# One softmax bias per query tile in place of one for the whole sequence, in a fused attention and feed-forward kernel

## The chip, the cores and the metric

The kernel runs on all eight cores of one Trainium2 chip, each core on its own sequence of the batch of eight; the cores exchange nothing. The metric is the device time in microseconds (us) of the slowest core.

## What is computed

One layer in pre-norm order: a causal attention with 16 heads of 64, then a feed-forward block with ternary weights, activations quantised per token, and a depthwise convolution of width 3 between the two products. The parts that matter here are the attention and the order of the two:

```python
# x: (8, 2048, 1024)
def attn(x, W_query, W_key, W_value):        # H = 16, DH = 64
    q, k, v = (heads(x @ W) for W in (W_query, W_key, W_value))
    scores = jnp.einsum('bhqd,bhkd->bhqk', q, k)
    scores = jnp.where(causal, scores, -jnp.inf)
    weights = jax.nn.softmax(scores / jnp.sqrt(jnp.float32(DH)), axis=-1)
    return merge(jnp.einsum('bhqk,bhkd->bhqd', weights, v))

x = x + attn(_layernorm(x), W_query, W_key, W_value)
x = x + ffn(_layernorm(x), w1, conv_w, conv_b, w2)
```

A softmax doesn't change when the same number is subtracted from all the scores of a query. The kernel subtracts a bound on the scores, so that the exponentials stay finite, and never looks for a row's true maximum.

## The kernel before, in words

The program is written out in full, without loops on the chip. Small functions marked `sec_t`, `sec_v`, `sec_s`, `sec_g`, `sec_sq` and `sec_gq` each append instructions to one engine (PE, DVE, ACT, POOL, the SyncE DMA queue, the GpSimd DMA queue), and each engine runs its list in the order written. All instructions go through the helper `emit` (line 75), so nearly every row of the profile carries that line and is told apart by its tile. On DVE, ACT and POOL `emit` also makes each instruction wait until the one before it on the same engine is complete:

```python
        if self.chain and self.n > 0:
            self.wait((self.sem, self.n))
```

The stages are:

1. Projections. 16 tiles of 128 rows of x are normalised (on ACT a pair Ln, Exp of one column of `smalls` gives the reciprocal root) and transposed, and Q, K and V are made into `qT`, `kT` and `vaug`, which stay in SBUF.
2. Norms and the bias (lines 465 to 555). For Q (`wix` 0) and K (`wix` 1) and each of four blocks `n` of 512 tokens, DVE squares the block into `sqb` in two halves, PE sums it over channels into one row of `psN`, and a `tensor_reduce` writes the block's largest squared norm into `nrm`, column `8 * wix + n`. Then a serial chain makes one number: two reductions over the four blocks, a product, Ln and Exp on ACT (a square root), two small `tensor_scalar` on DVE (times 0.125, at most 80, negated), a matmul with a row of ones that spreads it over 128 partitions of `psN`, and a `tensor_copy` into column 6 of `smalls` (token `expbias`).
3. Attention. For four query tiles `t` of 512 rows and eight head pairs `hp`: `emit_sc` puts the scores of a key chunk `kc` into `psS` (PE), `emit_exp1` turns them into `PT` (ACT, with `bias=smalls[:, 6:7]`, after a wait on `expbias` in `exp_pvwaits`), DVE masks the diagonal chunks, and `flush_pv` runs the product with V of the head pair before (`psPV`) and adds the result to `x1st`. After each head pair `emit_wsteps(2)` appends two steps of the work on the weights: sums of absolute values on ACT (`mk_w1_abs`, `mk_w2_abs`: a 1 MB load into one of the two halves of `wbuf`, then an Abs on ACT; load `i` waits for Abs `i - 2`), and after those the ternary quantisation on DVE.
4. Feed-forward. After a barrier on all that went before, eight groups of 256 tokens go through `psM`, the convolution (`tmpc`, `cbuf`), the sigmoid, the quantisation (`amx`, `hsil`, `hq`) and `psO`.

On PE the order around the change is: the norm matmuls of `sqb`, the matmul that spreads the bias (`psN<-nrm,onesrow_s`), and behind it the first scores `psS` of t = 0, hp = 0. On ACT it is: the last Ln and Exp of stage 1, Ln and Exp of the bias, the four exponentials of t = 0, hp = 0, two Abs of `wbuf`.

Of the kernel before, what the change touches and what calls it, by code (L numbers as in the profile page):

```python
# [10 lines left out]
AF = mybir.ActivationFunctionType  # L11
ALU = mybir.AluOpType
AX = mybir.AxisListType
# [9 lines left out]
NQT = S // QTW  # L23
# [108 lines left out]
def build_program(debug=False):  # L132
# [23 lines left out]
    dbg = {}  # L156
# [15 lines left out]
    with es:  # L172
# [11 lines left out]
        onesrow = es.enter_context(nc.sbuf_tensor("onesrow_s", [1, 128], F32))  # L184
        convw = es.enter_context(nc.sbuf_tensor("convw_s", [128, 96], F32))
        convb = es.enter_context(nc.sbuf_tensor("convb_s", [128, 32], F32))
        smalls = es.enter_context(nc.sbuf_tensor("smalls", [128, 64], F32))
# [262 lines left out]
        with esA2:  # L450
# [67 lines left out]
                            "tensor_reduce", nrm[0:1, col:col + 1],  # L518
                            psN[0:1, 0:512], AX.X, ALU.max)

            @sec_v
            def _(ve):
                VE.emit("tensor_reduce", nrm[0:1, 16:17], nrm[0:1, 0:4],
                        AX.X, ALU.max)
                VE.emit("tensor_reduce", nrm[0:1, 17:18], nrm[0:1, 8:12],
                        AX.X, ALU.max)
                toks["c2"] = VE.emit(
                    "tensor_tensor", nrm[0:1, 18:19], nrm[0:1, 16:17],
                    nrm[0:1, 17:18], ALU.mult)

            @sec_s
            def _(se):
                SE.wait(toks["c2"])
                SE.emit("activation", out=nrm[0:1, 19:20],
                        in_=nrm[0:1, 18:19], func=AF.Ln)
                toks["cval"] = SE.emit(
                    "activation", out=nrm[0:1, 20:21],
                    in_=nrm[0:1, 19:20], func=AF.Exp, scale=0.5)

            @sec_v  # L540
            def _(ve):
                VE.wait(toks["cval"])
                VE.emit("tensor_scalar", nrm[0:1, 21:22], nrm[0:1, 20:21],
                        0.125, 80.0, ALU.mult, ALU.min)
                toks["negb"] = VE.emit(
                    "tensor_scalar_mul", nrm[0:1, 22:23], nrm[0:1, 21:22],
                    -1.0)

            @sec_t
            def _(te):  # L550
                TE.wait(toks["negb"])
                TE.emit("matmul", psN[:, 0:1], onesrow[0:1, :],
                        nrm[0:1, 22:23], start=True, stop=True)
                toks["negb_mm"] = TE.tok()

            @sec_v
            def _(ve):
                VE.wait(toks["negb_mm"])
                toks["expbias"] = VE.emit(
                    "tensor_copy", smalls[:, 6:7], psN[:, 0:1])  # L560

            if debug:
                @sec_v
                def _(ve):
                    toks["dbg_nb"] = VE.emit("tensor_copy", nrm[0:1, 32:39],
                                             nrm[0:1, 16:23])

                @sec_sq
                def _(sy):
                    SQ.emit("dma_start", out=dbg["d_nb"][0:1, 0:7],  # L570
                            in_=nrm[0:1, 32:39], waits=[toks["dbg_nb"]])

            def mk_w1_abs(i):
                c, hf = divmod(i, 2)
# [257 lines left out]
            for t in range(NQT):  # L832
# [4 lines left out]
                for hp in range(8):  # L837
# [28 lines left out]
                            toks[("sc", t, hp, kc)] = TE.tok()  # L866

                    def exp_pvwaits(t, hp, kc):
                        SE.wait(toks["expbias"])
                        if kc == 0:  # L870
                            if hp >= 2:
                                SE.wait(toks[("pv", t, hp - 2, 0)])
                                SE.wait(toks[("pv", t, hp - 2, 1)])
                            elif t >= 1:
                                SE.wait(toks[("pv", t - 1, 6 + hp, 0)])
                                SE.wait(toks[("pv", t - 1, 6 + hp, 1)])

                    def emit_exp1(t, hp, kc):
                        hpar = kc % 2

                        @sec_s
                        def _(se, t=t, hp=hp, kc=kc, hpar=hpar):
                            SE.wait(toks[("sc", t, hp, kc)])
                            exp_pvwaits(t, hp, kc)
                            c0 = max(0, (kc - 4 * t) * 128)
                            bP = psS[hpar]
                            src_ap = bP[:].rearrange(
                                "p (h w) -> p h w", w=QTW)[:, :, c0:QTW]
                            PTp = PT[:, (hp % 2) * 2 * PTW:
                                      (hp % 2 + 1) * 2 * PTW]  # L890
                            dst_ap = PTp.rearrange(
                                "p (h w) -> p h w", w=16 * 512)[
                                :, :, 512 * kc + c0:512 * (kc + 1)]
                            toks[("exp", t, hp, kc)] = SE.emit(
                                "activation", out=dst_ap, in_=src_ap,
                                func=AF.Exp, scale=0.125,
                                bias=smalls[:, 6:7])

                    def emit_exp2(t, hp, kc):
                        @sec_s  # L900
                        def _(se, t=t, hp=hp, kc=kc):
# [12 lines left out]
                            tok = SE.emit(  # L914
                                "activation", out=dst_ap, in_=src_ap,
                                func=AF.Exp, scale=0.125,
                                bias=smalls[:, 6:7])
                            toks[("exp", t, hp, kc)] = tok
                            toks[("exp", t, hp, kc + 1)] = tok

# [663 lines left out]
```

How the kernel before makes its waits and increments, by code:

```python
    def wait(self, tok):  # L52
        if tok is None:
            return
        if isinstance(tok, list):
            for t in tok:
                self.wait(t)
            return
        sem, val = tok
        if val <= 0:
            return
        key = id(sem)
        if self._waited.get(key, -1) >= val:
            return
        if not DRY[0]:
            self.raw.wait_ge(sem, val)
        self._waited[key] = val
# [1 line left out]
    def emit(self, name, *a, waits=(), **kw):  # L69
        if self.chain and self.n > 0:
            self.wait((self.sem, self.n))
        for t in waits:
            self.wait(t)
        if not DRY[0]:
            inst = getattr(self.raw, name)(*a, **kw)
            inst.then_inc(self.sem, 1)
        self.n += 1
        return (self.sem, self.n)
# [20 lines left out]
    def wait(self, tok):  # L99
        if tok is None:
            return
        if isinstance(tok, list):
            for t in tok:
                self.wait(t)
            return
        sem, val = tok
        if val <= 0:
            return
        key = id(sem)
        if self._waited.get(key, -1) >= val:
            return
        if not DRY[0]:
            self.raw.wait_ge(sem, val)
        self._waited[key] = val
# [1 line left out]
    def emit(self, name, *a, waits=(), **kw):  # L116
# [5 lines left out]
        if not DRY[0]:  # L122
            inst = getattr(self.raw, name)(*a, **kw)
            inst.then_inc(self.sems[j], 16)
        self.counts[j] += 16
```

## Time and profile before

| | us |
|---|---|
| two timed runs | 2157.40, 2158.38 (median 2157.89) |
| profiled execution, its own time | 2155.54 |
| its span on the slowest core (core 1) | 2154.0 |
| spans of the eight cores | 2140.8 to 2154.0 |
| stage 1, to the last V matmul | 0 to about 323 |
| stage 2, norms and bias | about 324 to 388 |
| stage 3, attention and weights | about 388 to 1005 |
| stage 4, feed-forward | about 1005 to 2154 |

All rows are of core 1 unless a number of another core is named, and times in them count from the start of its span. The profiled execution took 1.54 us more than the span. Its time is 2.35 us under the median of the timed runs.

### The profile page before, as it was taken

The page shows a single profiled execution, that of the slowest core. Times are in us where ns is not written, and L with a number is a line of the kernel's source. Part 1 is how long each engine was busy: PE and PEld are TensorE (multiplying, and loading weights), DVE is VectorE, ACT ScalarE, POOL GpSimd, SP SyncE. Part 2 cuts the span into 40 slices and gives each one's busy share as a digit, 9 for nine tenths or more (in the row PEclk, how much of TensorE's full clock was granted, in tenths as well). Part 3 has the DMA queues.
Part 4 walks back from the last instruction along what each step waited for, and adds up shares of the span by engine and source line. Part 5 has one row for each costly group of instructions (what it writes and reads, how often), then busy time and mean ns, then how long its engine had stood idle before and what let it go on. Part 6 is the DMA issues. An engine that isn't in the chain of part 4 may idle for free.

```text
span 2154.0 us, 23769 instructions; the slowest of 8 cores (2140.8 to 2154.0 us)
## 1 busy us (share of the span) xinstructions
PE 1084.5 (50%) x7038; PEld 596.5 (28%) x7038; DVE 1058.6 (49%) x2042; ACT 829.2 (38%) x904; POOL 280.9 (13%) x255
## 2 busy tenths in 40 slices
PE   0656784344454445550042437355273564757555
PEld 0322330122232222330031324233232332443422
DVE  1344434333345556653545646547455474666560
ACT  3100000677855556750243251542424514252612
POOL 0000000000000000000012312213113231242320
PEclk9977885555665556665566768788686786989887
DMA  7211002474444454436522321323203223142300
GB/s 233 63 39 40 20 1 78 157 233 159 160 114 130 135 174 147 140 130 200 188 88 88 108 69 59 102 75 105 91 20 127 89 72 95 61 136 78 118 20 20
DMA packets 108273, 224.03 MB, mean 104 GB/s; under 512 B 4593, under 2 KB 70258, under 8 KB 104050
## 3 DMA queue, kind: packets, MB, share of 16 engines
q1 hardware_dynamic: 94962, 172.18, 25.7%
q0 software_dynamic: 13184, 50.34, 6.8%
q8 instruction: 58, 0.95, 0.2%
q14 instruction: 69, 0.57, 0.1%
HBM read 188.94 MB, written 33.55 MB: 103 GB/s over the span
## 4 chain that ended last, share of the span: by engine, by line
DVE 34%; PE 22%; DMA 17%; ACT 14%; issue 10%; DVEq 1%; SPq 1%; ACTq 0%; POOL 0%; POOLq 0%
PE psQK L75 8%; DMA wbuf<-w1t 7%; PE psO L75 6%; DVE t1s L75 5%; DVE amx L75 5%; DVE hsil L75 4%; DVE smalls L75 4%; DMA wbuf<-w2t 4%; PE psM L75 3%; DMA x1t<-x1scr 3%; ACT hf L75 3%; DVE cbuf L75 3%; DVE tmpc L75 3%; ACT PT L75 3%; ACT hq L75 2%
## 5 line engine op out<-in xcount | busy, mean ns | idle before, releaser
L75 PE MATMUL psM<-xqT,t1b 128*128 128x258 bf16 x2048 | 324.3, 327 | 369.8 <-DVE cbuf L75 357.4
L75 ACT ACTIVATE PT<-psS,smalls 128x1024 bf16<-128x1024 f32 (+1 forms) x320 | 315.5, 986 | 179.8 <-PE psS L75 152.1
L75 PEld LDWEIGHTS psM<-xqT,t1b 128*128 128x128 bf16 x2048 | 230.2, 116 | 463.0 <-issue 401.0
L75 ACT ACTIVATE tmpc<-psM,convb_s,convw_s 128x256 f32<-128x256 f32 x256 | 144.5, 565 | 386.1 <-PE psM L75 257.1
L75 PE MATMUL psS<-qT,kT 64*128 64x512 bf16 x640 | 168.3, 532 | 218.1 <-ACT PT L75 218.1
L75 PE MATMUL psO<-t2T,hq 128*128 128x512 bf16 x1024 | 224.1, 381 | 34.7 <-ACT hq L75 34.7
L75 DVE SCALAR_TENSOR_TENSOR tmpc<-psM,convw_s,tmpc 128x256 f32<-128x256 f32 x256 | 123.7, 483 | 233.4 <-ACT tmpc L75 211.8
L75 POOL TENSOR_TENSOR hsil<-cbuf,hsil 128x1024 f32<-128x1024 f32 x64 | 150.6, 2353 | 537.5 <-ACT hsil L75 537.5
L75 PE MATMUL psPV<-vaug,PT 128*128 128x65 bf16 x2176 | 117.0, 237 | 69.2 <-DVE PT L75 69.2
L75 ACT ACT_TABLE_LOAD x26 | 33.4, 1283 | 288.8 <-DVE smalls L75 162.0
L75 PEld LDWEIGHTS psO<-t2T,hq 128*128 128x128 bf16 x1024 | 100.1, 98 | 157.3 <-issue 39.4
L75 DVE SCALAR_TENSOR_TENSOR cbuf<-psM,convw_s,tmpc 128x256 f32<-128x256 f32 x256 | 123.7, 483 | 27.1 <-DVE tmpc L75 0.5
L75 PEld LDWEIGHTS psPV<-vaug,PT 128*128 128x128 bf16 x2176 | 112.9, 128 | 83.7 <-issue 83.7
L75 PEld LDWEIGHTS psS<-qT,kT 64*128 64x128 bf16 x640 | 37.2, 99 | 334.5 <-issue 332.1
L75 DVE TENSOR_REDUCE amx<-hsil 128x256 f32<-128x8192 f32 x8 | 112.7, 14089 | 4.7 <-POOL hsil L75 3.9
L75 DVE TENSOR_SCALAR t1s<-wbuf,smalls 128x2048 bf16<-128x2048 f32 x32 | 41.2, 1286 | 130.5 <-DMA wbuf<-w1t 70.5
L75 ACT ACTIVATE smalls<-smalls 128x1 f32<-128x1 f32 x64 | 13.0, 203 | 229.5 <-DVE smalls L75 226.1
L75 DVE TENSOR_TENSOR hsil<-hsil,s2row 128x256 f32<-128x256 f32 x128 | 92.5, 723 | 14.1 <-DVE hsil L75 0.9
L75 POOL TENSOR_TENSOR hsil<-hsil,s2row 128x256 f32<-128x256 f32 x128 | 93.9, 734 | 40.6 <-DVE s2row L75 22.3
L75 ACT ACTIVATE hsil<-cbuf 128x1024 f32<-128x1024 f32 x64 | 67.6, 1057 | 54.3 <-DVE cbuf L75 52.1
L75 DVE SCALAR_TENSOR_TENSOR x1st<-psPV,recb,x1st 128x64 f32<-128x64 f32 x256 | 72.5, 283 | 27.5 <-DVE x1st L75 0.9
L123 POOL DMA_DIRECT2D x1scr<-x1st x4 | 3.0, 750 | 622.6 <-DVE PT L75 331.8
(80 smaller groups left out, 1159.5 us busy)
## 6 DMA issues: line engine op xcount, KB each, us to landing
t1b<-t1scr SPq DMA_DIRECT2D x64, 1024.0 KB, 5.6
wbuf<-w1t SPq DMA_DIRECT2D x32, 1024.0 KB, 6.6
wbuf<-w2t SPq DMA_DIRECT2D x32, 1024.0 KB, 6.0
xstage<-x POOLq DMA_DIRECT2D x16, 512.0 KB, 4.1
x1st<-x POOLq DMA_DIRECT2D x4, 2048.0 KB, 11.4
x1scr<-x1st POOLq DMA_DIRECT2D x4, 2048.0 KB, 9.8
t1scr<-t1s SPq DMA_DIRECT2D x16, 512.0 KB, 3.8
t2scr<-t1s SPq DMA_DIRECT2D x16, 512.0 KB, 3.2
```

The source lines that it names most:

```text
L75: inst = getattr(self.raw, name)(*a, **kw)
L123: inst = getattr(self.raw, name)(*a, **kw)
```

## The change

The single chain of stage 2 goes, and a function `emit_bias(t)` takes its place. It is called four times in a row, for t = 0 to 3, where the single chain stood, before the first score matmul of the attention. Each call makes a bias for one query tile, from the largest squared norm of Q in block t and the largest of K over blocks 0 to t (a running maximum in columns 24 to 27 of `nrm`). The four results go to columns 6, 14, 15 and 29 of `smalls`, and the exponentials of tile t wait for and use their own. Every call has its own cells in `nrm` and `psN`. Nothing else is moved. The part under `debug`, cut below, isn't built.

```diff
@@ -518,57 +518,61 @@
                             "tensor_reduce", nrm[0:1, col:col + 1],
                             psN[0:1, 0:512], AX.X, ALU.max)
 
-            @sec_v
-            def _(ve):
-                VE.emit("tensor_reduce", nrm[0:1, 16:17], nrm[0:1, 0:4],
-                        AX.X, ALU.max)
-                VE.emit("tensor_reduce", nrm[0:1, 17:18], nrm[0:1, 8:12],
-                        AX.X, ALU.max)
-                toks["c2"] = VE.emit(
-                    "tensor_tensor", nrm[0:1, 18:19], nrm[0:1, 16:17],
-                    nrm[0:1, 17:18], ALU.mult)
-
-            @sec_s
-            def _(se):
-                SE.wait(toks["c2"])
-                SE.emit("activation", out=nrm[0:1, 19:20],
-                        in_=nrm[0:1, 18:19], func=AF.Ln)
-                toks["cval"] = SE.emit(
-                    "activation", out=nrm[0:1, 20:21],
-                    in_=nrm[0:1, 19:20], func=AF.Exp, scale=0.5)
-
-            @sec_v
-            def _(ve):
-                VE.wait(toks["cval"])
-                VE.emit("tensor_scalar", nrm[0:1, 21:22], nrm[0:1, 20:21],
-                        0.125, 80.0, ALU.mult, ALU.min)
-                toks["negb"] = VE.emit(
-                    "tensor_scalar_mul", nrm[0:1, 22:23], nrm[0:1, 21:22],
-                    -1.0)
-
-            @sec_t
-            def _(te):
-                TE.wait(toks["negb"])
-                TE.emit("matmul", psN[:, 0:1], onesrow[0:1, :],
-                        nrm[0:1, 22:23], start=True, stop=True)
-                toks["negb_mm"] = TE.tok()
-
-            @sec_v
-            def _(ve):
-                VE.wait(toks["negb_mm"])
-                toks["expbias"] = VE.emit(
-                    "tensor_copy", smalls[:, 6:7], psN[:, 0:1])
-
-            if debug:
+            BCOL = [6, 14, 15, 29]
+
+            def emit_bias(t):
                 @sec_v
...
+                def _(ve, t=t):
+                    VE.wait(toks[("nrm_rd", 0, t)])
+                    VE.wait(toks[("nrm_rd", 1, t)])
+                    if t == 0:
+                        VE.emit("tensor_copy", nrm[0:1, 24:25],
+                                nrm[0:1, 8:9])
+                    else:
+                        VE.emit("tensor_tensor", nrm[0:1, 24 + t:25 + t],
+                                nrm[0:1, 23 + t:24 + t],
+                                nrm[0:1, 8 + t:9 + t], ALU.max)
+                    toks[("c2", t)] = VE.emit(
+                        "tensor_tensor", nrm[0:1, 44 + t:45 + t],
+                        nrm[0:1, t:t + 1], nrm[0:1, 24 + t:25 + t],
+                        ALU.mult)
+
+                @sec_s
+                def _(se, t=t):
+                    SE.wait(toks[("c2", t)])
+                    SE.emit("activation", out=nrm[0:1, 48 + t:49 + t],
+                            in_=nrm[0:1, 44 + t:45 + t], func=AF.Ln)
+                    toks[("cexp", t)] = SE.emit(
+                        "activation", out=nrm[0:1, 52 + t:53 + t],
+                        in_=nrm[0:1, 48 + t:49 + t], func=AF.Exp, scale=0.5)
+
+                @sec_v
+                def _(ve, t=t):
+                    VE.wait(toks[("cexp", t)])
+                    VE.emit("tensor_scalar", nrm[0:1, 56 + t:57 + t],
+                            nrm[0:1, 52 + t:53 + t], 0.125, 80.0,
+                            ALU.mult, ALU.min)
+                    toks[("negb", t)] = VE.emit(
+                        "tensor_scalar_mul", nrm[0:1, 60 + t:61 + t],
+                        nrm[0:1, 56 + t:57 + t], -1.0)
+
+                @sec_t
+                def _(te, t=t):
+                    TE.wait(toks[("negb", t)])
+                    TE.emit("matmul", psN[:, 2 + t:3 + t], onesrow[0:1, :],
+                            nrm[0:1, 60 + t:61 + t], start=True, stop=True)
+                    toks[("negb_mm", t)] = TE.tok()
+
+                @sec_v
+                def _(ve, t=t):
+                    VE.wait(toks[("negb_mm", t)])
+                    toks[("expbias", t)] = VE.emit(
+                        "tensor_copy", smalls[:, BCOL[t]:BCOL[t] + 1],
+                        psN[:, 2 + t:3 + t])
+
+            for t in range(NQT):
+                emit_bias(t)
+
 
             def mk_w1_abs(i):
                 c, hf = divmod(i, 2)
@@ -866,7 +870,7 @@
                             toks[("sc", t, hp, kc)] = TE.tok()
 
                     def exp_pvwaits(t, hp, kc):
-                        SE.wait(toks["expbias"])
+                        SE.wait(toks[("expbias", t)])
                         if kc == 0:
                             if hp >= 2:
                                 SE.wait(toks[("pv", t, hp - 2, 0)])
@@ -894,7 +898,7 @@
                             toks[("exp", t, hp, kc)] = SE.emit(
                                 "activation", out=dst_ap, in_=src_ap,
                                 func=AF.Exp, scale=0.125,
-                                bias=smalls[:, 6:7])
+                                bias=smalls[:, BCOL[t]:BCOL[t] + 1])
 
                     def emit_exp2(t, hp, kc):
                         @sec_s
@@ -914,7 +918,7 @@
                             tok = SE.emit(
                                 "activation", out=dst_ap, in_=src_ap,
                                 func=AF.Exp, scale=0.125,
-                                bias=smalls[:, 6:7])
+                                bias=smalls[:, BCOL[t]:BCOL[t] + 1])
                             toks[("exp", t, hp, kc)] = tok
                             toks[("exp", t, hp, kc + 1)] = tok
 
```

DVE, from the last reduction of the norms (`nrm<-psN`) to the first mask of the attention (`PT<-PT,mask_s`), before:

```order
L75 TENSOR_REDUCE nrm<-psN 1x1
L75 TENSOR_REDUCE nrm<-nrm 1x1 x2
L75 TENSOR_TENSOR nrm<-nrm 1x1
L75 TENSOR_SCALAR nrm<-nrm 1x1 x2
L75 COPY smalls<-psN 128x1
L75 TENSOR_TENSOR PT<-PT,mask_s 128x128 x8
```

and now:

```order
L75 TENSOR_REDUCE nrm<-psN 1x1
L75 COPY nrm<-nrm 1x1
L75 TENSOR_TENSOR nrm<-nrm 1x1
L75 TENSOR_SCALAR nrm<-nrm 1x1 x2
L75 COPY smalls<-psN 128x1
L75 TENSOR_TENSOR nrm<-nrm 1x1 x2
L75 TENSOR_SCALAR nrm<-nrm 1x1 x2
L75 COPY smalls<-psN 128x1
...
L75 TENSOR_TENSOR PT<-PT,mask_s 128x128 x8
```

The group of five rows that begins with two TENSOR_TENSOR stands three times (t = 1, 2, 3); the line of dots stands for the second and third of them. DVE gains 14 small instructions in all.

PE and ACT at the same place, as a difference (PE first: the matmul that spreads the bias, between the norms and the scores):

```order
 L75 MATMUL psN<-sqb,onesb_s 1x512 x64
-L75 MATMUL psN<-nrm,onesrow_s 128x1
+L75 MATMUL psN<-nrm,onesrow_s 128x1 x4
 L75 MATMUL psS<-qT,kT 128x512 x16
```

```order
 L234 UNCONDITIONAL_BRANCH
-L75 ACTIVATE nrm<-nrm 1x1 x2
+L75 ACTIVATE nrm<-nrm 1x1 x8
 L75 ACTIVATE PT<-psS,smalls 128x2x512
 L75 ACTIVATE PT<-psS,smalls 128x2x384
```

PE has three more small matmuls ahead of the first scores, and ACT six more one-element activations ahead of the first exponential. POOL and the SyncE queue are as before.

## Rows read from the trace of the kernel before

**Rows 1.** The page's chain that ended last, shares of the span by engine and tile.

```profile
DVE 34%; PE 22%; DMA 17%; ACT 14%; issue 10%; DVEq 1%; SPq 1%; ACTq 0%; POOL 0%; POOLq 0%
```

**Rows 2.** DVE in order of time, 383.5 to 389: start, duration, then the idle before it.

```profile
383.56 0.68 DVE L75 TENSOR_REDUCE nrm<-psN 1x1 f32<-1x512 f32 x1 [2.19 <-PE psN L75]
384.34 0.39 DVE L75 TENSOR_REDUCE nrm<-nrm 1x1 f32<-1x4 f32 x2
384.84 0.15 DVE L75 TENSOR_TENSOR nrm<-nrm 1x1 f32<-1x1 f32 x1
387.08 0.39 DVE L75 TENSOR_SCALAR nrm<-nrm 1x1 f32<-1x1 f32 x2 [2.09 <-ACT nrm L75]
388.34 0.16 DVE L75 COPY smalls<-psN 128x1 f32<-128x1 f32 x1 [0.88 <-PE psN L75]
```

**Rows 3.** ACT in order of time, 384 to 389.5.

```profile
385.12 1.28 ACT L75 ACT_TABLE_LOAD   x1 [108.80 <-DVE nrm L75]
386.41 0.49 ACT L75 ACTIVATE nrm<-nrm 1x1 f32<-1x1 f32 x2
388.95 1.11 ACT L75 ACTIVATE PT<-psS,smalls 128x1024 bf16<-128x1024 f32 x1 [2.04 <-PE psS L75]
```

**Rows 4.** PE in order of time, 383 to 389.

```profile
387.61 0.55 PE L75 MATMUL psN<-nrm,onesrow_s 1*128 1x1 f32 x2 [4.23 <-DVE nrm L75]
388.10 1.03 PE L75 MATMUL psS<-qT,kT 64*128 64x512 bf16 x4
```

**Rows 5.** ACT, then the SyncE queue, in order of time from 391.

```profile
392.53 1.91 ACT L75 ACTIVATE wbuf<-wbuf 128x2048 f32<-128x2048 f32 x1
394.35 0.19 ACT L75 ACTIVATION_READ_ACCUMULATOR wbuf<-wbuf 128x1 f32 x1
...
400.98 1.91 ACT L75 ACTIVATE wbuf<-wbuf 128x2048 f32<-128x2048 f32 x1 [0.77 <-DMA wbuf<-w1t]
...
394.62 12.58 SPq L123 DMA_DIRECT2D wbuf<-w1t  x4
```

**Rows 6.** DVE and ACT in order of time in stage 1, around one Ln and Exp.

```profile
257.06 0.15 DVE L75 TENSOR_SCALAR smalls<-smalls 128x1 f32<-128x1 f32 x1
258.03 0.16 DVE L75 SCALAR_TENSOR_TENSOR smalls<-smalls 128x1 f32<-128x1 f32 x1 [0.82 <-ACT smalls L75]
258.49 0.81 DVE L75 TENSOR_SCALAR lnstage<-xstage,smalls 128x1024 bf16<-128x1024 f32 x1 [0.30 <-DVE smalls L75]
...
257.36 0.50 ACT L75 ACTIVATE smalls<-smalls 128x1 f32<-128x1 f32 x2 [51.11 <-DVE smalls L75]
263.64 0.50 ACT L75 ACTIVATE smalls<-smalls 128x1 f32<-128x1 f32 x2 [5.79 <-DVE smalls L75]
```

**Rows 7.** ACT by groups, 0 to 1040: count, busy and mean ns, idle before.

```profile
L75 ACT ACTIVATE smalls<-smalls 128x1 f32<-128x1 f32 x36 | 7.3, 203 | 211.7 <-DVE smalls L75 209.7
...
L75 ACT ACT_TABLE_LOAD x3 | 3.8, 1283 | 188.4 <-DVE nrm L75 108.8 <-DVE smalls L75 64.2 <-DMA wstage<-wq 15.4
```

**Rows 8.** Busy time by stretch (PE, PEld, DVE, ACT, POOL), then granted clock, DMA share, GB/s.

```profile
380.00:388.00 8.00, 2.25 (x6) 0.79 (x6) 2.62 (x7) 1.69 (x3) 0.00 (x0) 0.50 0.00 0
388.00:400.00 12.00, 5.21 (x26) 1.50 (x27) 1.96 (x9) 10.14 (x12) 0.00 (x0) 0.50 0.28 96
440.00:460.00 20.00, 6.81 (x56) 3.03 (x56) 10.84 (x46) 17.07 (x19) 0.00 (x0) 0.50 0.69 248
388.00:1040.00 652.00, 285.39 (x2837) 153.04 (x2837) 311.22 (x715) 384.18 (x391) 7.09 (x12) 0.58 0.51 163
1040.00:2154.00 1114.00, 579.31 (x3240) 348.10 (x3240) 600.47 (x1088) 412.63 (x465) 263.41 (x221) 0.77 0.26 83
```

**Rows 9.** The chain that ended last, 1040 to 2154: shares by engine and tile.

```profile
by line: issue 11.5%; PE psO L75 11.4%; DVE amx L75 10.1%; DVE hsil L75 8.3%; PE psM L75 6.4%; DVE smalls L75 6.4%; ACT hf L75 5.5%; DMA x1t<-x1scr 5.2%; DVE tmpc L75 5.0%; DVE cbuf L75 5.0%; ACT hq L75 4.0%; ACT hsil L75 3.1%; ACT tmpc L75
```

**Rows 10.** Spans and mean granted TensorE clock by core; then cores 0 and 4 at the bias.

```profile
core 0: 2149.4 us, clock 0.715
...
core 4: 2145.1 us, clock 0.716
core 5: 2140.8 us, clock 0.716
...
383.68 0.39 DVE L75 TENSOR_REDUCE nrm<-nrm 1x1 f32<-1x4 f32 x2
...
386.15 0.39 DVE L75 TENSOR_REDUCE nrm<-nrm 1x1 f32<-1x4 f32 x2
```

More of the change, by code:

```diff
@@ L549, in _ @@
-            @sec_t
-            def _(te):
-                TE.wait(toks["negb"])
-                TE.emit("matmul", psN[:, 0:1], onesrow[0:1, :],
-                        nrm[0:1, 22:23], start=True, stop=True)
-                toks["negb_mm"] = TE.tok()
-            @sec_v
-            def _(ve):
-                VE.wait(toks["negb_mm"])
-                toks["expbias"] = VE.emit(
-                    "tensor_copy", smalls[:, 6:7], psN[:, 0:1])
-            if debug:
-                @sec_v
[L564 to L571, printed above, removed]
+            BCOL = [6, 14, 15, 29]
```

## The prediction, written before the changed kernel ran

> **What bounds the kernel now.** I read first the page's chain that ended last [rows 1]. It is spread over DVE, PE, DMA and ACT, none above 34%: the kernel is a relay in which one engine hands to the next, and no engine has a queue of work that would hide a delay. So the question is local: at the place of the change, is the work on that relay, and does anything after it run by a time of its own?
>
> Next I read each engine in order of time at the bias. DVE ends the last norm reduction at 384.24 and starts the old chain at 384.34 [rows 2]. ACT had been idle for 108.80 us when it takes the chain up at 385.12 [rows 3]; PE was idle for 4.23 us before the matmul that spreads the bias at 387.61, and starts the first scores at 388.10, directly behind it [rows 4]; the first exponential starts at 388.95, having waited for the scores [rows 3]. From 384.34 to 388.95 exactly one engine works at a time, each named as the releaser of the next. The whole chain is on the path, 4.6 us. Only the last copy into `smalls` (388.34 to 388.50) has 0.45 us to spare, because the scores are longer.
>
> **The change, part by part.** *First bias (t = 0).* Two reductions and a product become a copy and a product. The two reductions start at 384.34 and the product at 384.84 [rows 2], so one such step is 0.25 us with its self-wait. One step fewer: -0.25 us.
>
> *Three more biases.* Each further chain starts on DVE only after the copy of the chain before it, since DVE runs its list in order and that copy is written first. So the chains can't overlap, although the numbers they need are all there at 384.24. One round costs, start to start:
> - copy into `smalls` to the running maximum: one DVE step, 0.25
> - running maximum to product: one DVE step, 0.25
> - product to Ln: 384.84 to 385.12, 0.28 in front of the table load [rows 2, 3]; without a load in front it is 257.06 to 257.36, 0.30 [rows 6]. I take 0.28
> - Ln to the first `tensor_scalar`, over Exp: 386.41 to 387.08, 0.67 [rows 2, 3]; the same in stage 1, 257.36 to 258.03 [rows 6]
> - the two `tensor_scalar` to the matmul: 387.08 to 387.61, 0.53 [rows 2, 4]
> - matmul (it shows as two passes, 0.55 in all) to the copy: 387.61 to 388.34, 0.73 [rows 2, 4]
>
> The sum is 0.25 + 0.25 + 0.28 + 0.67 + 0.53 + 0.73 = 2.71 us a round, and 8.13 us for three.
>
> Every operation in a round has a row of before at the same shape; only the maximum has none of its own, and is taken as the product beside it, also a `tensor_tensor` on one element (0.15 us). Bounds for a round: up, DVE once needs 0.46 us from step to step in stage 1 (258.03 to 258.49) where the chain shows 0.25 [rows 6]; with that at each of the four times that a DVE instruction of a round waits for the one before it, it is 2.71 + 4 x 0.21 = 3.55. Down, if the 0.18 us between the end of the matmul (387.61 + 0.55) and the copy (388.34) were nothing, 2.53. I take 2.71, since it is made of the rows at this very place; the ends give 7.6 and 10.65 for three.
>
> *What stands behind it on each engine.* On PE the first scores of t = 0 are queued behind all four spreading matmuls, and on ACT the first exponential behind all eight Ln and Exp. Before, the time from the matmul to the first exponential was 388.95 - 387.61 = 1.34 us; it stays so after the last of them. The bias for t = 0 is ready early and nobody can use it. The waits on `("expbias", t)` in the attention then cost nothing: all four biases are complete before the first exponential could start.
>
> *The table load.* ACT loads a table once, at 385.12, and then runs Ln, Exp and all the exponentials of the attention with it: only three loads stand between 0 and 1040, one in each of stages 1, 2 and 4, although stage 1 has 16 pairs Ln, Exp [rows 7], which follow one another without a load [rows 6]. So I count no further load.
>
> *Does the delay reach the end?* The work that could be waiting on something else is the loading of `w1t`. Its first two loads have been in since stage 2. The next is issued at 394.62, when the first Abs is through (394.35 + 0.19), and the Abs of its data starts at 400.98 [rows 5]. That Abs is queued on ACT behind the first four exponentials, so the loads move with the bias. The DMA share is 0.00 from 380 to 388 [rows 8]: there is no transfer in flight that would be waited for anyway. All later stages hang on attention, and stage 4 on a barrier. Nothing is hidden.
>
> *Clock.* The granted clock is 0.50, the lower level (1.2 GHz), in the 8 us before the attention and still at 440 to 460 [rows 8]. A longer pause of PE at this place has nothing to take away.
>
> **Sum.** 3 x 2.71 - 0.25 = +7.9 us. The profiled execution took 2155.54 and would take 2163.4; the median of the timed runs is 2.35 above it, so 2157.89 + 7.9 = 2165.8 us, 0.37% slower. A measurement of this kernel tells about 2% (43 us) from no change, so this would read as the same.
>
> **Rivals.**
>
> *A. Absorbed.* The attention could give the 8 us back: in 388 to 460 the stage is paced partly by loads (DMA share 0.69, 248 GB/s [rows 8]), and a delay before a bandwidth-paced stretch costs nothing where the transfers run on. For it: the cores reach the bias at different times (the two reductions start at 383.68 on core 0 and at 386.15 on core 4), and the later one has the shorter span, 2145.1 against 2149.4 [rows 10]. Against: only two loads can run ahead of ACT, and both have been there long before. Time: +0 to +4, so 2157.9 to 2162. Chance 0.10.
>
> *B. A table load at every switch.* If Ln and Exp of the short chains were given different tables, each of the four chains would have two loads where there is one now: 7 more of 1.283 us [rows 7], all on the path since ACT is waited for, 9.0 us on top. Time: 2157.89 + 7.9 + 9.0 = 2174.8. Against it: the 16 pairs of stage 1. Chance 0.03. The Trainium skill (ScalarE: Activation LUTs, "Table sets: the hidden batching unit") speaks of one set that holds exp alone among others and a second that holds both exp and ln; a choice function by function would then switch, and "What ACT_TABLE_LOAD costs" there prices a switch at about 2.66 us with its drain. By that estimate seven switches would be 18.6 us. The trace disagrees on both: it shows pairs without a load, and at the one load here ACTIVATE starts at 386.41, 0.01 us after the load ends.
>
> *C. Slower by over 2%: the clock of the feed-forward stage.* The mechanism is that all that follows starts later against the chip's other activity, and the clock granted from 1040 on comes out lower. There PE holds 11.4% + 6.4% of a chain of 1114 us, 198 us [rows 9], at a mean granted clock of 0.77 [rows 8]. To add 35 us to the 7.9 (43 in all) the clock would have to come down to c with 198 x (0.77 / c - 1) = 35, so c = 0.654. At the 0.58 of the attention stage [rows 8] it would be 65 us and 2230.7 in all. Against it: the cores reach the bias up to 2.5 us apart and their clocks are 0.715 and 0.716 [rows 10]. Chance 0.02.
>
> *D. The pattern of transfers falls differently.* The same program gives spans from 2140.8 to 2154.0 on cores with equal work [rows 10]. A shift may move the slowest core by a part of that 13 us in either direction, without any single cause. Time: 2157.9 + 7.9 with 5 either way, beyond the forecast's own. Chance 0.10.
>
> **How the numbers follow.** The forecast, the full delay, has 0.75 and its own range, 2163 to 2170 (7.6 - 0.25 and 10.65 - 0.25 on top of 2157.89 give 2165.2 and 2168.3; the two timed runs differ by 1, the profiled one from them by 2). A and D pull the range to 2158 below; B, and D upward, to 2175 above. Faster by over 2% would need a gain of 43 us, for which no row speaks: 0.01. Slower by over 2% is C and a little for the unseen: 0.02. The rest, 0.97, is within 2%.
>
> **What would show it right or wrong.** In the trace after, ACT should show one table load and eight `nrm` activations, in pairs 2.7 us apart; PE four pairs of `psN<-nrm,onesrow_s` at the same distance with idle between them named DVE `nrm`; and the first `PT` about 13.3 us after the start of the last `nrm<-psN` (5.4 in before, 383.56 to 388.95, and 7.9 more). The stretch from the first `PT` to the end should be as long as before, within the few us that cores differ. The prediction is wrong if the pairs are closer than 2.5 or wider than 3.5 us, if a table load stands between them, or if that later stretch has changed by more than 5 us: then the sum at the bias doesn't decide the time.

## The result, and the profile after

The changed kernel took 2167.13 us (median of 43 executions); before, run on the same chips, took 2153.81 (42 executions). The ratio is 1.0061, with an interval of 1.0045 to 1.0077, that is +13.1 us (9.7 to 16.6) where +7.9 was forecast. The time lies in the range that was forecast and the direction is as forecast; the size of the step is off by 5 us. The two executions of before that the forecast started from, 2157.4 and 2158.4, were above the median of what came later, so that the forecast of 2165.8 us lies nearer to the measured time, by luck, than the forecast step does to the measured step. (A part of the executions of either kernel is up to 1.6% longer, at a lower granted clock on some cores; the ratio leaves most of them out.)

At the bias the trace shows what the working said. ACT in order of time on core 3, the slowest of the changed kernel (start, duration, then the idle before it; compare [rows 3]):

```profile
387.04 1.28 ACT L75 ACT_TABLE_LOAD   x1 [110.26 <-DVE nrm L75]
388.34 0.50 ACT L75 ACTIVATE nrm<-nrm 1x1 f32<-1x1 f32 x2
391.08 0.49 ACT L75 ACTIVATE nrm<-nrm 1x1 f32<-1x1 f32 x2 [2.25 <-DVE nrm L75]
393.82 0.50 ACT L75 ACTIVATE nrm<-nrm 1x1 f32<-1x1 f32 x2 [2.24 <-DVE nrm L75]
396.56 0.49 ACT L75 ACTIVATE nrm<-nrm 1x1 f32<-1x1 f32 x2 [2.24 <-DVE nrm L75]
399.04 1.11 ACT L75 ACTIVATE PT<-psS,smalls 128x1024 bf16<-128x1024 f32 x1 [1.98 <-PE psS L75]
```

One table load, four pairs of Ln and Exp, 2.74 us from one to the next (2.71 in the sum), ACT idle for 2.24 of each. DVE (compare [rows 2]) and PE (compare [rows 4]) show the rest of a round:

```profile
385.74 0.68 DVE L75 TENSOR_REDUCE nrm<-psN 1x1 f32<-1x512 f32 x1 [2.19 <-PE psN L75]
386.52 0.14 DVE L75 COPY nrm<-nrm 1x1 f32<-1x1 f32 x1
386.76 0.15 DVE L75 TENSOR_TENSOR nrm<-nrm 1x1 f32<-1x1 f32 x1
389.01 0.39 DVE L75 TENSOR_SCALAR nrm<-nrm 1x1 f32<-1x1 f32 x2 [2.10 <-ACT nrm L75]
390.27 0.16 DVE L75 COPY smalls<-psN 128x1 f32<-128x1 f32 x1 [0.87 <-PE psN L75]
390.53 0.40 DVE L75 TENSOR_TENSOR nrm<-nrm 1x1 f32<-1x1 f32 x2
```

```profile
389.54 0.55 PE L75 MATMUL psN<-nrm,onesrow_s 1*128 1x1 f32 x2 [3.98 <-DVE nrm L75]
392.28 0.55 PE L75 MATMUL psN<-nrm,onesrow_s 1*128 1x1 f32 x2 [2.19 <-DVE nrm L75]
...
398.25 1.03 PE L75 MATMUL psS<-qT,kT 64*128 64x512 bf16 x4
```

From the start of the last norm reduction to the first exponential it is 399.04 - 385.74 = 13.30 us, against 383.56 to 388.95 = 5.39 in before [rows 2, 3]: +7.9, on every one of the eight cores. So the rest of the +13 is somewhere else. To find it, I took marks from each core's rows and averaged the stretches between them over the eight cores of the profiled execution (us):

| stretch | before | after | pad64 | pad17 | defer | early |
|---|---|---|---|---|---|---|
| start to the last V copy | 323.0 | 324.4 | 324.0 | 322.9 | 323.1 | 323.6 |
| last V copy to the first `PT` | 65.8 | 73.7 | 66.1 | 65.4 | 65.3 | 19.9 |
| first `PT` to the store of tile 0 | 76.9 | 77.3 | 76.0 | 77.3 | 77.0 | 77.4 |
| to the store of tile 3 | 510.6 | 510.8 | 509.3 | 510.6 | 512.4 | 511.3 |
| to the first `psM` matmul | 99.9 | 100.1 | 99.4 | 99.7 | 100.3 | 100.3 |
| first `psM` matmul to the end | 1072.1 | 1075.0 | 1071.0 | 1074.2 | 1076.5 | 1074.5 |

(The names are those of the experiments below.) Between the first `PT` and the first `psM` matmul the two differ by 0.8 us. The feed-forward stage is 2.9 us longer, though the change doesn't touch it. Stage 1, which it doesn't touch either, is 1.4 us longer, and that is how far such a mean differs from one execution to the next: stage 1 is the same code in before, after, defer and early (323.0 to 324.4), and in pad64 and pad17 it has only idle-time additions (324.0 and 322.9). One pair of profiles alone therefore doesn't show that the 2.9 us are real; the experiments do.

### The profile page after: what moved, and what is told of

It is laid out like the page before. It is cut to its first block, busy times and chain, and to the rows that moved or that the text cites. A ratio compares the mean times of both kernels' runs of the same rounds, so it can differ in the third digit from the quotient of the medians.

```text
span 2165.7 us, 23833 instructions; the slowest of 8 cores (2156.3 to 2165.7 us)
## 1 busy us (share of the span) xinstructions
PE 1092.7 (50%) x7044; PEld 598.6 (28%) x7044; DVE 1061.5 (49%) x2056; ACT 830.6 (38%) x910; POOL 280.9 (13%) x255
## 4 chain that ended last, share of the span: by engine, by line
DVE 33%; PE 21%; DMA 18%; ACT 14%; issue 10%; DVEq 1%; SPq 1%; ACTq 0%; POOL 0%; POOLq 0%
PE psQK L75 8%; DMA wbuf<-w1t 7%; PE psO L75 6%; DVE t1s L75 5%; DVE amx L75 5%; DVE hsil L75 4%; DMA wbuf<-w2t 4%; DVE smalls L75 4%; ACT hf L75 3%; DVE tmpc L75 3%; DVE cbuf L75 3%; DMA x1t<-x1scr 3%; ACT PT L75 3%; PE psM L75 2%; ACT hq L75 2%
## 5 line engine op out<-in xcount | busy, mean ns | idle before, releaser
L75 PE MATMUL psM<-xqT,t1b 128*128 128x258 bf16 x2048 | 333.0, 333 | 361.7 <-DVE cbuf L75 353.5
L75 PEld LDWEIGHTS psM<-xqT,t1b 128*128 128x128 bf16 x2048 | 234.7, 119 | 459.2 <-issue 392.8
L75 PE MATMUL psPV<-vaug,PT 128*128 128x65 bf16 x2176 | 112.5, 233 | 69.1 <-DVE PT L75 69.1
L75 PEld LDWEIGHTS psO<-t2T,hq 128*128 128x128 bf16 x1024 | 100.3, 98 | 159.6 <-issue 42.1
L75 PEld LDWEIGHTS psPV<-vaug,PT 128*128 128x128 bf16 x2176 | 108.3, 125 | 83.7 <-issue 83.7
L75 DVE TENSOR_SCALAR t1s<-wbuf,smalls 128x2048 bf16<-128x2048 f32 x32 | 41.2, 1286 | 127.0 <-DMA wbuf<-w1t 65.8
L75 DVE TENSOR_TENSOR hsil<-hsil,s2row 128x256 f32<-128x256 f32 x128 | 93.2, 728 | 13.3
```

The costliest lines, as they stand in the source:

```text
L75: inst = getattr(self.raw, name)(*a, **kw)
```

## The experiments

Each kernel was timed beside before on the same chip. Two numbers are given for each: the ratio of the times with its interval, and, since half a per cent is at stake, the difference of the mean over all eight cores' spans (+-: its standard error), over the executions that lie within 0.6% of the fastest of their kernel. The intervals of the ratios are wide: those of again, seven, samecol, batch and defer overlap, and those of pad17, pad64, act8 and defer47 all hold 1. What tells these kernels apart is the means and the traces. Four chips were used, one for again, seven, samecol and batch, a second for defer and early, a third for pad17, pad64, after47 and early50, a fourth for act8 and defer47. The mean of before is 2145.8 to 2150.5 us on them, so kernels on different chips are compared only through their difference to before.

**again.** The changed kernel as it is.

> The changed kernel once more, beside before on this chip. Theory L (the delay at the bias, passed on one to one): first exponential 13.3 us after the start of the last norm reduction (5.4 in before), total +7.9 us. Rival G (what is lost at the bias grows on its way, as the median of +13 suggests): the same 13.3 us at the bias, total about +13. Rival R (a fixed loss of about 5 us elsewhere, from the per-tile bias operand or from where the code lies): the same 13.3 and about +13 too; the other runs tell G from R.

Measured: 1.0056 (1.003 to 1.0083); mean of the cores +11.9 +- 0.6 us. The excess over 7.9 is there again, 4 us. L, which said +7.9, doesn't hold as it stands.

**seven.** Does the loss grow with the delay?

```diff
-            for t in range(NQT):
-                emit_bias(t)
+            for k in range(7):
+                emit_bias(k)
```

(Not shown: `emit_bias(k)` for k = 4 to 6 makes t = 1 to 3 again, with its own tokens and columns.)

> Seven rounds in a row in place of four: the rounds of tiles 1 to 3 are made twice, the second time into columns that nothing reads. L: 3 x 2.74 more than the changed kernel at the bias, first exponential 21.5 us after the start of the last norm reduction, total +16.1 us over before. G: 16.1 x 13/7.9 = +26. R: +16 + 5 = +21.

Measured: 1.0059 (1.0028 to 1.009); mean of the cores +16.3 +- 0.7 us. The first exponential starts 21.5 us after the last norm reduction. Here the total is the local delay (21.5 - 5.4 = 16.1) and nothing else: with a first exponential at 13.3 us there is an excess of 4, with one at 21.5 none. Theory G (+26) is out, and R (+21) too, as far as it means one fixed loss in every kernel with the change.

**samecol.** One bias column for all tiles (the exponentials of tiles 0 to 2 use the bias of tile 3, not their own).

```diff
-                                bias=smalls[:, BCOL[t]:BCOL[t] + 1])
+                                bias=smalls[:, BCOL[3]:BCOL[3] + 1])
```

> Four rounds as in the change, but all exponentials read the one column of the last query tile, so that each has the same bias operand as in before. L: +7.9 us. R, where it is the per-tile operand: +7.9, against +13 of the changed kernel in the same call. G: +13, as the changed kernel.

Measured: 1.0055 (1.0029 to 1.0082); mean of the cores +13.7 +- 0.6 us. The excess stays (5.8 us here; its attention is 2.6 us longer than that of the changed kernel in the profiled execution), so it isn't the bias operand.

**batch.** The four biases in one chain, four elements wide.

```diff
-            for t in range(NQT):
-                emit_bias(t)
...
+                toks["c2"] = VE.emit(
+                    "tensor_tensor", nrm[0:1, 44:48], nrm[0:1, 0:4],
+                    nrm[0:1, 24:28], ALU.mult)
...
+                SE.emit("activation", out=nrm[0:1, 48:52],
+                        in_=nrm[0:1, 44:48], func=AF.Ln)
...
+                TE.emit("matmul", psN[:, 2:6], onesrow[0:1, :],
+                        nrm[0:1, 60:64], start=True, stop=True)
```

> The four biases in one chain on rows of four elements (copy, three maxima, one product, one Ln, one Exp, two tensor_scalar, one matmul of four columns, one copy); per-tile bias as in the change. L: the product starts two DVE steps of 0.25 us later than in before, first exponential 5.9 us after the start of the last norm reduction, total +0.5 us. G: +0.8. R, where it is the per-tile operand or the code: +5.5.

Measured: 1.0029 (0.9999 to 1.0059); mean of the cores +0.7 +- 0.4 us. The first exponential starts 5.9 us after the last norm reduction. The per-tile biases cost half a microsecond when they are made in one round. DVE in order of time in this kernel on core 1 shows why: the 5.39 us of before plus two steps of 0.25, for the five small instructions that stand where three stood.

```profile
386.65 0.14 DVE L75 COPY nrm<-nrm 1x1 f32<-1x1 f32 x1
386.90 0.91 DVE L75 TENSOR_TENSOR nrm<-nrm 1x1 f32<-1x1 f32 x4
389.91 0.42 DVE L75 TENSOR_SCALAR nrm<-nrm 1x4 f32<-1x4 f32 x2 [2.10 <-ACT nrm L75]
391.21 0.16 DVE L75 COPY smalls<-psN 128x4 f32<-128x4 f32 x1 [0.88 <-PE psN L75]
```

**defer.** The rounds of tiles 1 to 3 cut into pieces and put behind head pairs 1 to 5 of tile 0.

```diff
-            for t in range(NQT):
-                emit_bias(t)
+            emit_bias(0)
...
+            late = {
+                (0, 1): ([(late_c2, 1)], [(late_sqrt, 1)]),
+                (0, 2): ([(late_neg, 1), (late_c2, 2)],
+                         [(late_bc, 1), (late_sqrt, 2)]),
...
```

> Norms as in the change, the first round ahead of the attention, the rounds of tiles 1 to 3 in pieces, one behind each of the head pairs 1 to 5 of tile 0, where ACT waits for loads part of the time. L: first exponential 5.15 us after the start of the last norm reduction, total -0.25 us plus at most the 6 x 0.25 us that the late Ln and Exp take on ACT: between -0.3 and +1.2. A rival (a late piece holds the engine that waits in order behind it) has up to 2.2 us for each of the three rounds back: up to +6.

Measured: 1.0041 (1.0001 to 1.0082); mean of the cores +7.3 +- 0.8 us. The first exponential starts 5.15 us after the last norm reduction, so the 8 us at the bias are gone, the attention takes 2 us more (589.4 against 587.5), and yet the total is +7: the feed-forward stage is 4.4 us longer (the table above). A kernel without the delay has the excess, one with the largest delay (seven) has none.

**What the excess is.** The step from the seventh to the eighth `amx` reduction in the feed-forward stage is 103.9 us in before, in seven and in early, and 104.6 in the changed kernel, in again, samecol and defer, and in none of these kernels do two of the eight cores differ by more than 0.1 us in it. Transfers or neighbours that get in the way would hardly cost every core the same 0.7 us. The chain of waits of before on core 0, after the seventh `amx` reduction (start, duration, what; "issue" is time in which the engine waited for nothing that the profile shows):

```profile
1972.62 0.17 DVE amc L75
1972.80 0.03 issue
1972.83 0.02 DVEq L66
1972.85 0.05 issue
1972.89 0.16 DVE amc L75
1973.06 0.03 issue
1973.08 0.02 DVEq L66
1973.11 0.05 issue
1973.15 0.17 DVE amc L75
```

and the same instructions in the changed kernel, on the same core:

```profile
1985.78 0.17 DVE amc L75
1985.96 0.03 issue
1985.99 0.02 DVEq L66
1986.01 0.05 issue
1986.05 0.16 DVE amc L75
1986.22 0.03 issue
1986.25 0.02 DVEq L66
1986.27 0.40 issue
1986.66 0.16 DVE amc L75
```

Between the last two, a pause of 0.40 us stands where 0.05 stood, and nothing is waited for. (A second one like it is in the same step, between two waits in the convolution; each adds 0.36 us, together they are the 0.7 us.) Counting the entries of DVE's stream in the trace from 0 (instructions and waits, each its own entry), the pause lies behind entry 4666 in the changed kernel, and 4666 = 58 + 36 x 128. So I looked at the gap behind every entry of the form 58 + 128 k, that is, the time from its end to the start of the next entry, on core 0:

```
kernel    DVE entries  more by    of the form 58 + 128 k: count, with a gap of 0.36 to 0.48 us
before    4939         -          39, 23
after     4973         34         39, 23
seven     5009         70         39, 20
```

and of the 128 places in a period only this one has a median gap above 0.1 us; it is 0.40, and the typical gap is 0.04. The other places are not without the pause; it is hidden there. Over all 14 traces (13 kernels, the changed one twice) and all cores, 2552 of these places hold a wait, and behind not one of them is the gap under 0.39 us. 960 hold an instruction longer than 0.42 us, and the gap behind it is as a rule the usual 0.04. Behind a shorter instruction, the instruction and the gap together come to about 0.40 us (0.16 and 0.23, 0.21 and 0.20, 0.28 and 0.11 on core 0 of before). So the pause runs beside an instruction that is under way, and is seen in full only behind a wait. In before, entry 4666 is the convolution instruction at 1985.60, and the step to the next is 0.59 us like the one ahead of it; the pause costs nothing there:

```profile
1985.01 0.48 DVE L75 SCALAR_TENSOR_TENSOR tmpc<-psM,convw_s,tmpc 128x256 f32<-128x256 f32 x1
1985.60 0.48 DVE L75 SCALAR_TENSOR_TENSOR cbuf<-psM,convw_s,tmpc 128x256 f32<-128x256 f32 x1
1986.19 0.48 DVE L75 SCALAR_TENSOR_TENSOR tmpc<-psM,convw_s,tmpc 128x256 f32<-128x256 f32 x1
```

In the changed kernel the same entry number falls on the wait between two `amc` instructions, where it is seen. ACT's stream shows it at the same place of its own period, with a median of 0.32 in the changed kernel; of 1444 waits that stand there in the 14 traces, none has a gap under 0.31. The change adds 34 entries to DVE ahead of all that follows, and so each pause of the later stages falls 34 entries earlier in the work. Some fall behind a wait on the path, others behind an instruction that hides them. That is theory S, and it can be tried without touching the bias.

**pad17, pad64.** Before, with memsets of one unused column on DVE while it waits for the V matmuls of stage 1. A memset with its self-wait is two entries. (The edit of pad17; pad64 has 64 for 17.)

```diff
                             st = 4 * sb + ms
+                            k = 8 * sb + j
+                            for _i in range(17 * (k + 1) // 32
+                                            - 17 * k // 32):
+                                VE.emit("memset", smalls[:, 64:65], 0.0)
                             VE.wait(toks[("qkv_mm", sb, 2, j)])
```

> The kernel before with 17 memsets of one column added on DVE while it waits for the V matmuls of stage 1: 34 entries more in DVE's instruction stream with their self-waits, as many as the change adds, and no added work on the path. Theory S (DVE pauses about 0.40 us at every 128th entry of its stream, at entries 58, 186, 314 and so on in all traces so far; what stands ahead decides on which instruction of the later stages each pause falls): pauses still at 58 + 128 k, the step from the 7th to the 8th amx reduction 104.6 us as in the changed kernel and not 103.9 as in before, the stretch from the first psM matmul to the end 1074 to 1076 us on average over the cores, not 1072, total +3 to +5 us. Rival (the excess over 7.9 comes from the delay or from the per-tile code): step 103.9, total 0.

Measured: 1.0008 (0.9988 to 1.0028); mean of the cores +3.6 +- 0.6 us. The step is 104.6 us, on all cores, the pause lies behind entry 4666, ahead of the same instruction as in the changed kernel, and the feed-forward stage is 1074.2 us. Stage 1, where the memsets run, takes 322.9 us, so they cost nothing themselves. In the time of the slowest core (1.0008) the effect doesn't show.

> The same with 64 memsets, 128 entries more: one whole period, so every pause falls on the same instruction as in before. S: step from the 7th to the 8th amx reduction 103.9 us, total -0.5 to +1 us. Rival (any added instructions cost, wherever they stand): more than pad17, +5 us or more.

Measured: 1.0009 (0.9982 to 1.0037); mean of the cores -0.1 +- 0.8 us. Nearly four times as many memsets cost nothing, and the step is 103.8 us. What counts is the position in the period of 128 and not the number of instructions.

**after47.** The changed kernel with 47 memsets: 34 + 94 entries, one period.

> The changed kernel with 47 such memsets, 94 entries more: with the 34 of the change one whole period over before. S: step 103.9 us, and the total over before falls from +12 to the delay at the bias alone, +7.9 (between +7 and +9). Rival: +12 or more as in the changed kernel.

Measured: 1.0031 (0.9999 to 1.0064); mean of the cores +4.8 +- 0.7 us. The step is 103.8 us and the first exponential still 13.3 us after the last norm reduction. The 12 us have fallen by 7, more than the 4 that S says, to under the +7 to +9 expected. The feed-forward stage takes 1071.6 us, and the attention is 2 us shorter than in before; but it is so in pad64 too, whose total is that of before. Where the missing 3 us went isn't shown.

**act8.** ACT's stream alone moved.

```diff
                             in_=smalls[:, 5:6], func=AF.Exp, scale=-0.5)
+                        k = st - 4
+                        for _i in range(8 * (k + 1) // 12 - 8 * k // 12
+                                        if k >= 0 else 0):
+                            SE.emit("activation", out=smalls[:, 65:66],
+                                    in_=onesf[:, 0:1], func=AF.Identity)
```

> The kernel before with 8 one-column activations added on ACT in stage 1, each behind the Ln and Exp of its tile where ACT is idle: 16 entries more in ACT's stream, DVE's as in before. Theory S for ACT too (ACT pauses at every 128th entry as well, and the change moves ACT's entries by 15): total +1 to +4 us over before, most of it between the first exponential and the last amx reduction. Rival (ACT's pauses lie in its waits, only DVE's count): 0 +- 1 us.

Measured: 1.0002 (0.9976 to 1.0028); mean of the cores +0.2 +- 1.0 us. A shift of ACT's pauses by 16 entries, with DVE's where they were, changes nothing that this shows; S for ACT had said +1 to +4.

**defer47.** The kernel defer with 47 memsets on DVE and 55 activations and a wait on ACT in stage 1, so that DVE's stream is a period (128 entries) behind before's and ACT's nearly so: it comes out at 127 entries in the trace, one short.

> The kernel with the rounds of tiles 1 to 3 behind head pairs, with 47 memsets on DVE and 55 one-column activations and one wait on ACT, all in stage 1 where the engines are idle, so that both streams lie one whole period behind those of before. S: the +7 us of that kernel falls to what was expected of it first, between -0.3 and +1.2 us over before. Rival (a late round holds up the attention): the total stays above +4.

Measured: 0.9996 (0.997 to 1.0023); mean of the cores -2.0 +- 0.8 us. The +7.3 of defer becomes -2.0 (on another chip, each beside before) by instructions that do nothing. The rival, a late round that holds up the attention and keeps the total above +4, is out.

**early, early50.** Only the norms of block 0 and the first round stay ahead of the attention. A norm block n of a later tile goes between two head pairs, its squares into `sqb` and the still unused `t1s` ahead of the masks, its matmuls behind the product with V, its reduction one head pair later: the blocks of tile 1 in tile 0, those of tiles 2 and 3 in tile 1. That each query tile has its own bias is what allows this.

```diff
-            for wix, buf in ((0, qT), (1, kT)):
-                for n in range(4):
+            for n in range(1):
+                for wix, buf in ((0, qT), (1, kT)):
...
+            late = {
+                (0, 1): ([(late_sq, 0, 1)], [(late_mm, 0, 1)]),
+                (0, 2): ([(late_rd, 0, 1), (late_sq, 1, 1)],
+                         [(late_mm, 1, 1)]),
+                (0, 3): ([(late_rd, 1, 1), (late_c2, 1)], [(late_sqrt, 1)]),
...
```

> Only the norms of block 0 of Q and K and the first round stand ahead of the attention; the six other norm blocks and the rounds of tiles 1 to 3 run in pieces between the head pairs of tiles 0 and 1. Six norm blocks of 7.6 us each (330.3 to 383.6 for seven steps in before) leave the path: if PE and DVE have the time free there, -45 us, first exponential at about 343 instead of 389. A rival: the squares (2 x 1.23 us) and the matmuls (3.7 us) of a block delay masks and scores that ACT waits for, and 2 to 6 us of each block come back: -10 to -33 us. A second rival, that the loads of w1t bound tile 0 anyway so that an earlier start gains nothing: they are issued behind ACT, so this gives -45 too.

Measured: 2113.79 us, ratio 0.9786 (0.9741 to 0.983); mean of the cores -42.2 +- 0.6 us. The stretch from the last V copy to the first `PT` falls from 65.8 to 19.9 us, and the first tile of the attention, which now also holds two of the eight norm blocks, takes 77.4 where it took 76.9. DVE in order of time in tile 0 (core 1) shows where the work went:

```profile
348.12 1.21 DVE L75 TENSOR_TENSOR PT<-PT,mask_s 128x128 bf16<-128x128 bf16 x4 [0.22 <-ACT PT L75]
349.44 1.23 DVE L75 TENSOR_TENSOR sqb<-qT 128x2048 bf16<-128x2048 bf16 x1
350.77 1.22 DVE L75 TENSOR_TENSOR t1s<-qT 128x2048 bf16<-128x2048 bf16 x1
356.61 0.18 DVE L75 RECIPROCAL recb<-psPV 128x4 f32<-128x4 f32 x1 [4.62 <-PE psPV L75]
...
362.94 0.68 DVE L75 TENSOR_REDUCE nrm<-psN 1x1 f32<-1x512 f32 x1
```

Even with the squares done, DVE waits 4.62 us for PE. ACT's longest waits in this tile are for the loads, 6.6 us in all (9.1 in before); for the late norms it waits 0.5 us, once:

```profile
350.74 1.91 ACT L75 ACTIVATE wbuf<-wbuf 128x2048 f32<-128x2048 f32 x1
...
352.84 3.50 ACT L75 ACTIVATE PT<-psS,smalls 128x1024 bf16<-128x1024 f32 x4
357.59 1.91 ACT L75 ACTIVATE wbuf<-wbuf 128x2048 f32<-128x2048 f32 x1 [1.26 <-DMA wbuf<-w1t]
```

early50 has 50 memsets more on DVE, placed as in pad17, for 28 + 100 entries.

> The kernel with the norms of the later tiles moved into the attention, with 50 such memsets, 100 entries more: with its own 28 one whole period over before. S: the stretch from the first psM matmul to the end falls from 1074.5 to about 1072 us, total about -44 us over before where it was -42. Rival: -42 or less.

Measured: 2110.12 us, ratio 0.9784 (0.9745 to 0.9822); mean of the cores -44.8 +- 1.0 us. The feed-forward stage falls from 1074.5 to 1070.1 us. The ratios of the two can't be told apart, and their step from the seventh to the eighth `amx` is the same 103.9 us; the stage and the means differ, the means on two chips. Both beat before and the changed kernel.

**All kernels, by the shift alone.** The mean over the cores of the stretch from the first `psM` matmul to the end, in every profiled execution. The cores of a kernel scatter by about 2 us, so each mean is good to about 0.7.

| DVE entries more than before in stage 4 | kernels | us |
|---|---|---|
| 0 or 128 | before, act8, pad64, after47, defer47, early50 | 1070.1 to 1072.4 |
| 34 | the changed kernel, again, samecol, defer, pad17 | 1074.2 to 1076.5 |
| 4 | batch | 1070.8 |
| 28 | early | 1074.5 |
| 70 | seven | 1073.2 |

The first two rows don't overlap, and their averages are 3.7 us apart, though each row has kernels with one bias and with four, with and without the delay, from several chips. The granted clock of the stage is 0.767 in the first row and 0.765 in the second, which by rival C's sum (198 us of PE) is worth 0.5 us.

## Why the prediction was right, and where its size was off

- *The chain is on the path, and the rounds can't overlap.* Right: 2.74 us a round against 2.71, 13.30 us to the first exponential against 13.3 forecast, with no other engine at work in between. Seven rounds gave 3 x 2.74 us more, and one wide round (batch) took the cost away.
- *One DVE step fewer in the first round, -0.25.* Right: defer, which has only that, starts its exponentials 5.15 us after the reduction, before 5.39.
- *No further table load.* Right: one in front of eight activations. Rival B, with +9.0, is out. Since no switch happened, no run prices one, and the one load came after 110 us in which ACT was idle, so it doesn't show what a busy ACT would pay; "the trace disagrees" with the higher price goes too far in rival B.
- *Nothing is hidden (rival A).* Right: the w1t loads moved with the bias (on core 3 the next one is issued at 404.71, behind the first Abs; at 394.62 in before), and the first tile took 77.3 us against 76.9.
- *Clock (rival C).* The granted clock of stage 4 is 0.764 on average of the cores in the profiled execution against 0.767 in before, which by C's own sum (198 us of PE) is worth 0.8 us and not 35; C is out.
- *"The stretch from the first `PT` to the end should be as long as before."* This is the term that was mis-sized. The stretch came out 3.7 us longer, within the few us that the prediction allowed it, where the sum had nothing. The sum costed added instructions only where they run. They also shift the places at which DVE pauses in every later stage, worth +3.6 us here (pad17), of the 4 to 5 that were missing. With this term the sum is 7.9 + 3.6 = 11.5, against 11.9 +- 0.6 measured in again and a ratio that gives 9.7 to 16.6. The time of 2167.13 us is also within rival D's 5 us either way, but D's reason (transfers falling differently on single cores) wasn't the one: the excess is in the mean of all cores. That the range held is in part luck: the starting value was 4 us above the median of what came later, and from that value a step of 13.1 would have ended at 2171, outside of 2163 to 2170.
- The pause was in the rows, unread: the step of 258.03 to 258.49 that served as an upper bound for a DVE step [rows 6] begins with entry 442, and 442 = 58 + 3 x 128. There an instruction of 0.16 us and 0.23 of the pause are most of what the prediction took as its upper bound for a step.

What stays open: the kernels that lie a whole period behind before while having other work at the bias come out 2 to 3 us below their sum (after47 4.8 for 7.9, defer47 -2.0 for -0.3 to +1.2), and defer is 3.7 us above pad17 with the same shift of DVE, on another chip, which ACT's shift alone (act8, +0.2) doesn't explain. No run shifts both streams as defer does without its late rounds. Nor does any run show what the engine does in the pause. The Trainium skill (Runtime: NRT & Kernel Launch, "Instruction fetch mechanics") describes code as being loaded in blocks of 256 instructions and the crossing from block to block as mostly hidden; the period measured here is 128 entries of the trace, and behind a wait the 0.40 us are in plain sight. Whether it is the same thing isn't shown; if it is, the measurement decides.

## What to carry to other kernels

A serial chain through three engines costs its hand-overs, not its arithmetic: four one-element rounds took 8 us more than one, and one round four elements wide took 0.5 us more. A value that is needed per tile is worth having per tile only when what feeds it moves as well: the change made four biases in the same place and lost 12 us, and the same four biases, with their norms moved to where the engines were idle, gained 42 to 45 (mean of the cores). When a few microseconds in a long unrolled program don't add up, compare stretches that the change doesn't touch across the cores; a difference that was the same on all of them to 0.1 us was a shift of the instruction stream here. Do-nothing instructions in an idle place test it: one number of them that reproduces the shift, and one that completes the period.

## What was not expected of the hardware

DVE holds the entry behind every 128th of its stream (58, 186, 314 and so on) back for 0.40 us (the median), in all 13 kernels here alike. Behind a wait this is seen in full, and behind an instruction longer than 0.42 us as a rule not at all; ACT does the same with 0.32 us at the same places of its own stream. In a program of 4939 DVE entries that is 39 pauses, 14 us if each were seen with its 0.36 us over the usual gap. What the path sees of it depends on how many entries stand ahead. Adding 34 entries that cost nothing where they run made the mean of the cores 3.6 us longer, and adding 128 made it no longer.
